# A convolution-attention layer and a selective-scan layer: softplus as one activation, the order of the scan stage moved, loops written out, the last stage with four buffers and four row groups

## The reference, cut to what matters

```python
x = jnp.transpose(x_hsi, (0, 2, 3, 1)).reshape(B_, H * W, C)
xh, z = jnp.split(x @ W_in, 2, axis=-1)                  # 256 channels each
xh = silu(_causal_conv_k2(xh, conv_w, conv_b))
x_dbl = xh @ W_x                                         # dt_low, Bmat, Cmat
dt = softplus(dt_low @ W_dt + b_dt)
# per position, for 16 states n:
h = exp(dt * A) * h + dt * Bmat * xh
y = (h * Cmat).sum(n)
out = ((y + xh * D) * silu(z)) @ W_out
x = silu(_group_norm(out, gn_gamma, gn_beta)) + x_hsi
```

## Time and profile before

| what | value |
|---|---|
| median of 3 runs | 17306.35 us (17305.44 to 17314.31) |
| the profiled execution | 17308.57 us |
| its span in the trace | 17306.8 us |
| stage A | about 0 to 2440 us |
| stage F and set-up of B | about 2440 to 2540 us |
| stage B | about 2540 to 16627 us |
| stage C | about 16627 to 17307 us |
| mean granted TensorE clock | 0.886 of full |

### The profile page before, as it was taken

The page is one execution under the profiler, slowest core; times in us unless marked ns, Lnnn a source line. Parts: engine busy times, 40 slices in busy tenths (PEclk is TensorE's granted clock), DMA queues, the critical chain, the costliest instruction groups (busy, mean ns, idle before and its releaser), DMA issues. The chain is left out here.

```text
span 17306.8 us, 188395 instructions
## 1 busy us (share of the span) xinstructions
PE 14501.2 (84%) x40250; PEld 5566.1 (32%) x40250; DVE 14618.9 (84%) x14056; ACT 10286.0 (59%) x14202; POOL 13647.4 (79%) x5903
## 2 busy tenths in 40 slices
PE   8999978888888888888888888888888888888876
PEld 3444433333333333333333333333333333333322
DVE  1222239999999999999999999999999999999942
ACT  2222236666666666666666666666666666666642
POOL 0000019999999999999999999999999999999930
PEclk9999988888888888888888888888888888888865
DMA  1111114444444444444444444444444444444445
GB/s 52 38 41 40 43 42 159 159 160 161 161 162 160 157 159 159 160 162 160 162 160 160 156 159 160 162 160 162 160 160 156 159 160 162 160 162 160 160 186 209
DMA packets 508191, 2499.22 MB, mean 144 GB/s; under 512 B 53097, under 2 KB 164938, under 8 KB 226651
## 3 DMA queue, kind: packets, MB, share of 16 engines
q1 hardware_dynamic: 489723, 2419.71, 37.7%
q10 hardware_dynamic: 18208, 76.11, 1.2%
HBM read 2325.05 MB, written 170.57 MB: 144 GB/s over the span
## 5 line engine op out<-in xcount | busy, mean ns | idle before, releaser
L734 POOL TENSOR_TENSOR hc<-h,c_all 128x1024 f32<-128x1024 f32 x4096 | 9526.1, 2354 | 287.9 <-PE y_ps L975 283.2
L975 PE MATMUL y_ps<-hc,ident 128*128 128x512 f32 x16392 | 8032.1, 635 | 900.2 <-POOL hc L734 899.5
L850 ACT ACTIVATE d_a<-dt,a_neg 128x512 f32<-128x512 f32 x8194 | 5596.4, 688 | 4243.9 <-DVE h L1079 4195.4
L1079 DVE TENSOR_TENSOR_SCAN h<-d_a,h,dbx_v 128x512 f32<-128x512 f32 x4960 | 6087.2, 1264 | 25.1
L975 PEld LDWEIGHTS y_ps<-hc,ident 128*128 128x128 f32 x16392 | 3185.3, 203 | 5870.4 <-issue 3862.9
L723 POOL TENSOR_TENSOR dbx_p<-dtx,b_all 128x1024 f32<-128x1024 f32 x1536 | 3613.9, 2353 | 168.4 <-DVE h L1079 168.1
L1079 DVE TENSOR_TENSOR_SCAN h<-d_a,h,dbx_p 128x512 f32<-128x512 f32 x2976 | 3654.0, 1262 | 42.2 <-ACT d_a L850 36.3
L1066 DVE TENSOR_TENSOR dbx_v<-dtx_ps,b_all 128x1024 f32<-128x1024 f32 x2560 | 3013.3, 1201 | 12.9 <-issue 9.3
L479 POOL MEMSET ident_f<- 128x128 f32 x1 | 0.2, 204 | 2438.4 <-POOLq L44 2438.4
L272 PE MATMUL conv_ps<-image,w_taps 128*32 128x512 f32 x11520 | 1785.0, 595 | 0.0
L984 PE MATMUL p_ps<-y,w_out 128*128 128x512 f32 x1028 | 889.8, 1017 | 1020.7 <-DVE dt L1106 1019.4
(11 more groups left out here) (129 smaller groups left out, 10823.4 us busy)
## 6 DMA issues: line engine op xcount, KB each, us to landing
b_all<-bc_dram SPq DMA_DIRECT2D x1028, 1024.0 KB, 6.9
c_all<-bc_dram SPq DMA_DIRECT2D x1025, 1024.0 KB, 4.7
o_dram<-o_sb SPq DMA_DIRECT2D x257, 256.0 KB, 7.4
o_t<-o_dram SPq DMA_DIRECT2D x64, 1024.0 KB, 9.6
out<-r_t ACTq DMA_DIRECT2D x64, 1024.0 KB, 9.2
image<-in_x SPq DMA_DIRECT2D x91, 512.0 KB, 4.1
un<-un_dram SPq DMA_DIRECT2D x516, 34.0 KB
bc_dram<-low_bc SPq DMA_DIRECT2D x257, 64.0 KB, 4.6
```

The lines of the kernel that those rows point to most:

```text
L734: nc.gpsimd.tensor_tensor(hc[:, n % HC], h[:, n], c_all[:, n // CG % 2, n % CG].unsqueeze(1).broadcast_to([128, 2, CH]), ALU.mult).then_in ...
L850: nc.scalar.activation(d_a[:, half], dt[:, p, half], ACT.Exp, scale=a_neg[:, half, n:n + 1]).then_inc(a_done, 1)
L975: last = nc.tensor.matmul(y_ps[:, half], ident[:], hc[:, n % HC, half], start=False, stop=(n == S - 1))
L1079: nc.vector.tensor_tensor_scan(h[:, n, half], d_a[:, half], dbx, zero_col[:] if first else h[:, n, half, CH - 1:CH], ALU.mult, ALU.add).th ...
```

## The change

Softplus becomes one activation for each half, between two table loads, and writes dt itself; the three DVE steps and ACT's `absolute`, `exponential`, `plus_one`, `logarithm`, `biased` go. State 14 moves from POOL to DVE. The orders of ACT, DVE, POOL and PE within a chunk change. In stages A, B and C hardware loops become loops of the program's author (`for b in range(0, B)`), so that their instructions stand written out and their waits are against constants. Stage C is rewritten with four buffers for o, u and the result; u lies as four pieces of 512 columns at partitions 0, 32, 64 and 96, the matrices of all batches lie below them, and scale and shift are read in place.

```diff
-                    with sp.Fori(0, PIECES - 3) as j:
+                    for j in range(0, PIECES - 3):
...
-            with pe.Fori(0, B) as b:
+            for b in range(0, B):
...
-ON_POOL = [7, 9, 11, 13, 14, 15]
+ON_POOL = [7, 9, 11, 13, 15]
...
 # POOL, body
-                weigh(km, 7)
                 weigh_out(km, 0)
                 weigh_out(km, 1)
+                weigh_out(km, 2)
+                weigh(km, 7)
                 weigh(km, 9)
-                weigh_out(km, 2)
                 weigh_out(km, 3)
...
                 weigh_out(km, 11)
+                weigh(km, 15)
+                make_dtx(km, 1 - p)
                 weigh_out(km, 12)
...
 # ACT
-            def biased(km, half):
...
-            def logarithm(km):
...
+            def softplus(km, p):
+
+                after(act, "a_done", 2 * S * km)
+                after(act, "dtx_done", km)
+                for half in range(2):
+                    after(act, f"dt_mm{half}", km + 2)
+                    last = nc.scalar.activation(dt[:, p, half], p_ps[:, half], ACT.Softplus, bias=b_dt[:, half:half + 1])
+                last.then_inc(dt_done, 1)
+                nc.scalar.preload_act_table_set("natural_log_exp_and_others")
...
                 decay(km, 2, 1, p)
+                silu_x(km, q)
+                nc.scalar.preload_act_table_set("natural_log_exp_and_others")
                 decay(km, 3, 0, p)
...
-                silu_x(km, q)
                 decay(km, 5, 0, p)
...
                 decay(km, 10, 1, p)
-                exponential(km)
+                softplus(km, q)
                 decay(km, 11, 0, p)
...
                 decay(km, 12, 1, p)
+                copy_out(km)
...
                 decay(km, 15, 1, p)
+                copy_dtx(km, q)
                 decay(km + 1, 0, 0, q)
...
 # DVE, body
                 run_scan(km, 2, 1, first)
+                gate(km, q)
+                weigh(km, 4)
                 run_scan(km, 3, 0, first)
...
-                gate(km, q)
...
+                weigh(km, 14)
                 run_scan(km, 11, 0, first)
...
 # stage C
-        gm = sb("gm_c", [KU, B, C])
-        gm_b = sb("gm_b", [KU, 2, C])
-        o_t = sb("o_t", [C, 2, CB])
-        u_t = sb("u_c", [KU, 2, CB])
+        gm = sb("gm_c", [128, B, C])
+        o_t = sb("o_t", [C, CBUF, CB])
+        u_t = sb("u_c", [128, CBUF, CH])
...
+            for b, j, k in blocks:
+                s = k % CBUF
+                if k >= CBUF:
+                    sp.wait_ge(silu_done, k - CBUF + 1)
+                c0 = (b * NCH + 1) * CH + j * CB
+                sp.dma_start(o_t[:, s], o_dram[:, c0:c0 + CB]).then_inc(o_in[s], 16)
+                if k >= CBUF:
+                    sp.wait_ge(res_mm, k - CBUF + 1)
+                c0 = (b * SLOTS + 1) * CH + j * CB
+                for g in range(groups):
+                    sp.dma_start(u_t[32 * g:32 * g + KU, s], un_dram[:, c0 + g * CH:c0 + g * CH + CH]
+                                 ).then_inc(u_in[s], 16)
...
+                for g in range(groups):
+                    last = nc.tensor.matmul(res_ps[:, k % 2, CH * g:CH * g + CH], gm[32 * g:32 * g + KU, b],
+                                            u_t[32 * g:32 * g + KU, k % CBUF], start=True, stop=True)
+                last.then_inc(res_mm, 1)
```

More of the change, by code:

```diff
@@ L38 @@
 CB = 2048
+CBUF = 4
 NCB = N // CB
@@ L231, in query @@
                 act.dma_start(uq[M:KU, bass.ds(c0, CH)], s_sb[:, p]).then_inc(u_stored[p], 16)
-            with act.Fori(0, B) as b:
-                with act.Fori(0, NCH // 2) as j:
+            for b in range(0, B):
+                for j in range(0, NCH // 2):
                     for p in range(2):
@@ L412, in _ @@
                         next(between)(b - 1)
-                with dve.Fori(3, NCH // 2 - 1) as j:
+                for j in range(3, NCH // 2 - 1):
                     for i in range(2):
@@ L610, in chunks @@
         def chunks(eng, body):
-            with eng.Fori(0, B) as b:
+            for b in range(0, B):
                 body(b, b * NCH, b * (NCH // 2), 0, 0, True, False)
-                with eng.Fori(0, NCH // 2 - 1) as j:
+                for j in range(0, NCH // 2 - 1):
                     body(b, b * NCH + 2 * j + 1, b * (NCH // 2) + j, 2 * j + 1, 1, False, False)
@@ L684, in body @@
                 sp.dma_start(o_dram[:, bass.ds(km * CH, CH)], o_sb[:]).then_inc(o_stored, 16)
-            with sp.Fori(0, B) as b:
+            for b in range(0, B):
                 at = b * (SLOTS * CH) + CH
                 body(b, b * NCH, at + 2 * CH, 0, False)
-                with sp.Fori(0, NCH // 2 - 2) as j:
+                for j in range(0, NCH // 2 - 2):
                     for i in range(2):
@@ L1222, in phase_c @@
         added = sem("C_added")
-        stored = [sem(f"C_stored{p}") for p in range(2)]
+        stored = [sem(f"C_stored{s}") for s in range(CBUF)]
         block = ctx.enter_context(nc.Block())
+        blocks = [(b, j, b * NCB + j) for b in range(B) for j in range(NCB)]
+        groups = CB // CH
         @block.sync
@@ L1244, in _, with store @@
         @block.scalar
         def _(act):
+            def store(b, j, k):
+                act.wait_ge(added, k + 1)
+                act.dma_start(out[b, :, j * CB:j * CB + CB], r_t[:, k % CBUF]).then_inc(stored[k % CBUF], 16)
             act.wait_ge(step, STEPS_BEFORE_ROOT)
             nc.scalar.activation(g_std[:], g_m2[:], ACT.Sqrt, bias=eps[:]).then_inc(rooted, 1)
-            with act.Fori(0, B) as b:
-                act.wait_ge(ab_done, 2 * b + 2)
-                with act.Fori(0, NCB // 2) as j:
-                    for p in range(2):
-                        k = b * NCB + 2 * j + p
-                        act.wait_ge(o_in[p], 16 * (b * (NCB // 2) + j + 1))
-                        act.wait_ge(added, k + 1)
-                        nc.scalar.activation(act_t[:, p], o_t[:, p], ACT.Silu, bias=ab[:, 1, 0:1], scale=ab[:, 0, 0:1]
-                                             ).then_inc(silu_done, 1)
-                        act.wait_ge(added, k + 3)
-                        act.dma_start(out[bass.ds(b, 1), :, bass.ds((2 * j + p) * CB, CB)]
-                                      .rearrange("o c n -> (o c) n"), r_t[:, p]).then_inc(stored[p], 16)
@@ L1260, in _ @@
-            for p in range(2):
-                act.wait_ge(stored[p], 16 * (B * NCB // 2 + 1))
+            act.wait_ge(step, STEPS_BEFORE_USE)
+            for b, j, k in blocks:
+                act.wait_ge(o_in[k % CBUF], 16 * (k // CBUF + 1))
+                if k >= 2:
+                    store(*blocks[k - 2])
+                nc.scalar.activation(act_t[:, k % 2], o_t[:, k % CBUF], ACT.Silu, bias=shift[:, b:b + 1],
+                                     scale=scale[:, b:b + 1]).then_inc(silu_done, 1)
@@ L1263, in _ @@
+            store(*blocks[-2])
+            store(*blocks[-1])
+            for s in range(CBUF):
+                act.wait_ge(stored[s], 16 * (B * NCB // CBUF))
         @block.tensor
```

169 lines of the change are left out of this document (39 added, 130 removed).

## The result

| what | before | changed |
|---|---|---|
| median | 17307.02 us (17305.44 to 17314.31, 4 runs) | 16763.63 us (16756.45 to 16766.77, 4 runs) |
| span in the trace | 17306.8 us | 16762.5 us |
| stage A ends | 2438.4 us | 2416.3 us |
| first and last gate of stage B | 2557.8, 16617.7 us | 2521.2, 16036.8 us |

The ratio is 0.9685, with a 95% interval from 0.9668 to 0.9701. The forecast was 16390 us, with a range up to 16610: 373 us too low. The gates of DVE divide the gain. Up to the first gate the changed kernel is 36.6 us ahead. Between the first and the last gate it needs 13515.6 us in place of 14059.9, 544.3 less. From the last gate to the end it needs 725.7 us in place of 689.1, 36.6 **more**. So stage B came nearly as forecast, and the last stage, which was to bring 274 us, lost some.

A forecast was written before the change was run, and what follows sets the result against it. Stage B bound by DVE's own work, stage C by a chain of waits; 17308.6 - 630 (stage B) - 4 (ahead of first chunk) - 274 (stage C) - 10 (stage A), less 2.2, about 16390 us; range 16260 to 16610.

The forecast's parts named there:

- The step that failed: Stage C: DMA engines are what is left, 5.84 us per block, 6.1 with pieces; gain 274 us.
- The chain no longer binds: Stage C: with four buffers, alternating u loads and PE products no longer set the time, 10.42 us per block before.
- The piece term: Stage C: 0.3 us per block added for loading u in pieces of 2 KB.
- DVE's own work: Stage B: 32 scans, 12 operations on 1024 columns and one statistics, 51.91 us per chunk.
- The gate's waits: Stage B: DVE's gate waits for PE by up to half a microsecond in most chunks; chunk 52.3 against 51.9 us.
- The ring: Stage B: gate and scans on DVE, POOL's 14 instructions, PE's tail, then the next gate; 52.3 us per chunk.
- ACT's softplus block: Stage B: two table loads and two activations take 3.87 us and fit in time, 0.15 us to spare.
- Rival 1: Stage B: lower clock lasts 11 of 20 passes, chunk 53.9 us, gain 220 instead of 630, total 16800 us; chance 0.08.
- Rival 2: Stage C: row groups don't overlap, PE takes 7.2 us per block, gain 199, total 16465 us; chance 0.08.
- Rival 3: Stage B: a second 1.4 us behind each new table switch on ACT, 666 us lost, total 17055 us; chance 0.03.
- Rival 4: Stage B: PE stays at 1.2 GHz from pause to gate, 57.8 us per chunk, slower, total 17800 us; chance 0.03.
- Rival 5: Stage B: code fetches or softplus cost what DVE saves, only stages A and C gain, total 17020 us; chance 0.04.

The follow-up runs named there:

- experiment 3: The changed kernel, still with four buffers, but u in one load of 17 rows and no row groups; 16751.8 us, 12 less than the changed kernel.
- Experiment 2: The kernel before, with the load of u split into 16 rows and 1 row; 17111.43 us, ratio 0.9883.
- experiment 7: Changed kernel with u loaded as 16 and 1 rows (16420.7 us), plus POOL's product of state 11 moved behind state 15's dbx; 16323.13 us.
- experiment 8: Changed kernel with u loaded as 16 and 1 rows (16420.7 us), plus the gate one state later, behind state 3's scans; 16913.81 us.

## Why the prediction was wrong, and where it was right

- **The step that failed: "What is left is the DMA engines: 0.56 x 10.42 = 5.84 us per block now."** It took a mean over 16 engines for the demand on each. One engine carried the 17 rows of u and was busy for the whole block: 4 to 5 us of it at 26 GB/s, where nothing else moved. So with four buffers and row groups a block took 10.91 us in place of 6.1, and the stage lost 37 us where 274 were forecast: 311 of the 373 us. (Stage B has another 86, and up to the first gate 23 came back.) "The chain no longer binds" was right as far as it goes; the chain was the picture of a lone engine, seen through a load that lasted 13.26 us. The range had 7.2 as its upper end for the block, with PE; it had no case in which a single DMA engine decides.
- The piece term, "0.3 for u in pieces of 2 KB", comes to 0.1 in experiment 3. Of the 0.47 us by which a block grew, 10.91 - 10.44, the other 0.36 has no cause shown.
- Experiment 2 shows the same step from the other side: with the load spread the block of the kernel before falls from 10.44 to 7.36 us, with its two buffers. So the lone engine held it there too.
- **Stage B: 630 forecast, 544 measured.** DVE's own work was mis-sized: without the gate's 132.3 us of waits the changed kernel takes (13515.6 - 132.3) / 256 = 52.28 us per chunk, where the forecast counted 51.91. That is 94 us, in which smaller waits and longer chunks at the changes of batch are included. In experiment 7's kernel, where few gates wait, a plain chunk takes 52.14 (gates at 9014.65 and 9066.79).
- The gate's waits were put at 52.3 - 51.91 = 0.39 us per chunk, 100 us, and are 132. Against this the kernel before had chunks of 14059.9 / 256 = 54.92 us on the mean, not 54.76, which gives back 41: 94 + 32 - 41 = 85.
- The ring was right as a mechanism, and experiment 7 bears it out, but not in its form. The forecast had the gate late by up to half a microsecond in most chunks. In the trace 116 gates of 257 wait, for 0.86 us on the mean, and the others not at all, but for seven longer waits, one at the end and six at changes of batch. Tails of 4.1 and 5.0 are seen, and gates 52.13 (9017.74 to 9069.87) and 52.99 us (to 9122.86) apart: of the passes behind the pause some 4 are slow in one case and 6 to 7 in the other, and only the longer case waits. That 116 x 0.86 comes to the forecast's 100 us is luck.
- ACT's softplus block holds: 683 ns per activation, 1283 per table load, 5.2 us of idle time in all ahead of the block. The scans of DVE's own states wait for 8.8 us in the whole run.
- Stage A gained 22.1 us, forecast 10 (0 to 15). Kv's eight waits sum to 79.3 us, 56.7 of them the first load, so a change of batch costs 3.2 in place of 5.01: 12.6 us. PE is also busy for 6.4 us less there (2327.41 and 2320.97). The other 3 were not traced.
- Rival 1 (the ring binds harder, 53.9): no for the mean. Rival 2 (row groups don't overlap): no, PE takes 2.09 us per block. Rival 3: a second 1.4 us behind table switches isn't there: the softplus activations stood idle for 3.3 us in all 257 chunks. So the Trainium skill's drain (ScalarE: Activation LUTs, What ACT_TABLE_LOAD costs) is again not in the trace. Rival 4 (slower, clock): no. In experiment 8 passes at the lower clock are one link of a chain that costs 493 us; their share in it was not measured. Rival 5 had the wrong half: the change reached stage B and missed the last.
